# First expert layer of a two-layer graph network: order of the scatters, of SP's row loads and of the sort's lookups

## What is computed

```python
H = gelu(xf @ W1 + b1)                       # 6250 x 1024
probs = softmax(H @ Wg + bg)                 # 8 experts
assign = argmax(probs, axis=-1)
for e in range(8):
    y = H @ Wd[e] + bd[e]
    out = out + where(assign == e, probs[:, e:e+1] * y, 0)
```

## Time and profile before

| what | us |
|---|---|
| median of 3 runs | 10559.74 (10548.85 to 10565.69) |
| the profiled execution, its time | 10558.26 |
| its span in the profile | 10556.3 |
| of it: self-loops on POOL | 3936 to 4022 |
| groups | 4022 to 4888 |
| positions and rows into XS | 4888 to 4984 |
| tiles | 4984 to 6071 |

### The profile page before, as it was taken

The page is one execution under the profiler, slowest core; times in us unless marked ns, Lnnn a source line. Parts: engine busy times, 40 slices in busy tenths (PEclk is TensorE's granted clock), DMA queues, the critical chain, the costliest instruction groups (busy, mean ns, idle before and its releaser), DMA issues. The chain is left out here.

```text
span 10556.3 us, 132376 instructions
## 1 busy us (share of the span) xinstructions
PE 6743.9 (64%) x29670; PEld 5088.8 (48%) x29671; DVE 4968.9 (47%) x10855; ACT 3051.4 (29%) x7313; POOL 6031.6 (57%) x6341
## 2 busy tenths in 40 slices
PE   4674999999999755775777665555444463555530
PEld 2333666666666544664666634444333352344420
DVE  6875777777777774664444431111111121222224
ACT  1113666656666201111111113333333310111110
POOL 1223666666666106666444537777777716777763
PEclk8777999999999876776777777777777666777765
DMA  2115666666777332222444334443333322222214
GB/s 74 51 55 175 209 208 208 208 207 208 208 209 210 97 93 61 71 72 84 124 124 125 108 115 119 118 119 112 100 100 100 101 61 55 43 48 45 47 28 152
DMA packets 657558, 1228.01 MB, mean 116 GB/s; under 512 B 165551, under 2 KB 409475, under 8 KB 657254
## 3 DMA queue, kind: packets, MB, share of 16 engines
q0 software_dynamic: 301872, 718.92, 24.7%
q1 hardware_dynamic: 327959, 467.65, 14.1%
q10 hardware_dynamic: 27580, 39.79, 1.0%
HBM read 1088.88 MB, written 145.05 MB: 117 GB/s over the span
## 5 line engine op out<-in xcount | busy, mean ns | idle before, releaser
L948 POOL DMA_INDIRECT e_kv<-KV,e_idx x1712 | 1634.2, 955 | 756.2 <-issue 482.4
L2453 POOL DMA_INDIRECT s_x<-XN,s_idx x1712 | 1622.7, 948 | 589.8 <-issue 499.4
L1593 POOL DMA_INDIRECT SD<-o_pay,o_pos x1024 | 1077.8, 1053 | 806.7 <-DVEq L45 438.3
L2510 PE MATMUL s_psA<-s_x,s_oh 128*128 128x256 f32 x1712 | 665.0, 478 | 1112.7 <-DMA s_x<-XN,s_idx 1018.9
L2868 POOL DMA_INDIRECT t_g<-G,t_idx x1088 | 1077.1, 990 | 329.7 <-issue 329.7
L2546 DVE TENSOR_TENSOR NS<-s_psA,NS 128x256 f32 x856 | 363.4, 425 | 1743.9 <-PE s_psA L2511 1743.5
L1053 PE MATMUL e_psQ<-QA,e_oht 128*128 x3424 | 895.0, 407 | 200.5 <-issue 102.1
L2510 PEld LDWEIGHTS s_psA<-s_x,s_oh 128*128 128x128 f32 x1712 | 405.7, 245 | 1222.2 <-issue 1152.5
L1053 PEld LDWEIGHTS e_psQ<-QA,e_oht 128*128 128x128 f32 x3424 | 646.9, 199 | 368.9 <-issue 282.4
L3036 PE MATMUL t_psH<-t_xT,t_w 128*128 128x384 f32 (+1 forms) x1088 | 425.5, 558 | 379.0 <-ACT t_H L3013 358.5
L2511 PE MATMUL s_psA<-s_x,s_oh 128*128 128x256 f32 x1712 | 625.0, 453 | 0.0
(11 more groups left out here) (580 smaller groups left out, 12617.4 us busy)
## 6 DMA issues: line engine op xcount, KB each, us to landing
o_dbf<-DBF SPq DMA_DIRECT2D x128, 512.0 KB
f_w<-in_L_ffn_Wd_dram SPq DMA_DIRECT2D x57, 1024.0 KB
e_relb<-REL SPq DMA_DIRECT2D x107, 512.0 KB, 6.0
o_dlo<-DLO SPq DMA_DIRECT2D x128, 256.0 KB
e_kv<-KV,e_idx POOLq DMA_INDIRECT x1712, 3.9
s_x<-XN,s_idx POOLq DMA_INDIRECT x1712
YD<-t_y ACTq DMA_DIRECT2D x50, 512.0 KB, 2.7
mx_y<-YD SPq DMA_DIRECT2D x10, 2560.0 KB, 11.3
```

The costliest lines, as they stand in the source:

```text
L948: pool.indirect_dma_start(kv[:, s, t, :], None, k.KV, bass.IndirectOffsetOnAxis(ap=idx[:, s, t:t + 1], axis=0)).then_inc(kv_in[s][g], 16)
L1593: pool.indirect_dma_start(self.k.SD, bass.IndirectOffsetOnAxis(ap=self.pos[:, s, j:j + 1], axis=0), self.pay[:, s, j, :], None).then_inc(s ...
L2453: pool.indirect_dma_start(x[:, s, t, :], None, k.XN2, bass.IndirectOffsetOnAxis(ap=idx[:, s, t:t + 1], axis=0)).then_inc(x_in[s], 16)
L2510: pe.matmul(psA[:, u % 4, 0:C], oh[:, o, 2 * u, :], x[:, s, 2 * u, :], start=True, stop=False)
```

## The change

Four edits, all in `GatSort` and `first_experts`:

1. The 64 self-loop scatters leave `pool_start`. A new method `place(pool, t)` issues one of them; 7 are issued after the groups, one after each sort block of the 57 tiles. The wait for their landing moves to `pool_end`.
2. In the tile loop POOL issues `give(j-2)` ahead of the sort block's scatters rather than behind them. The loop is now 57 tiles written out, not a hardware loop (`place` takes its column at build time).
3. SP reads `xa` one tile earlier: `xa` of tile j+1 is asked for at the head of SP's work for tile j, ahead of the sort's broadcasts.
4. In a group the seven sort steps of PE stand after the transposes, after m = 1, 3, 5 and 7, within the logits (after the third of five node tiles) and after the logits; ACT's steps follow.

```diff
@@ -1582,10 +1582,10 @@
         for s in range(2):
             pool.dma_start(self.blank[:, s, 1:2], self.blank[:, s, 0:1]).then_inc(self.scattered[s], 16 * SB)
         pool.wait_ge(self.loops_done, 1)
-        for t in range(HG):
-            pool.indirect_dma_start(k.SD, bass.IndirectOffsetOnAxis(ap=k.start2_i[:, t:t + 1], axis=0),
-                                    self.loops[:, t, :], None).then_inc(self.placed, 16)
-        pool.wait_ge(self.placed, 16 * HG)
+
+    def place(self, pool, t):
+        pool.indirect_dma_start(self.k.SD, bass.IndirectOffsetOnAxis(ap=self.k.start2_i[:, t:t + 1], axis=0),
+                                self.loops[:, t, :], None).then_inc(self.placed, 16)
 
     def pool_step(self, pool, b, s):
         after(pool, self.pos_done, b)
@@ -1594,6 +1594,7 @@
                                     self.pay[:, s, j, :], None).then_inc(self.scattered[s], 16)
 
     def pool_end(self, pool):
+        pool.wait_ge(self.placed, 16 * HG)
         for s in range(2):
             pool.wait_ge(self.scattered[s], 16 * SB * (self.blocks // 2 + 1))
 
@@ -1844,16 +1845,22 @@
             sp.wait_ge(owner_done, 1)
             sp.wait_ge(sorted_, 16 * NT)
 
-            def fetch(j, s, e):
+            def load_xa(j, s):
                 at(sp, xb_done, j - 2, 1, 0)
                 sp.dma_start(xa[:, s, :], rows(k.XS, j)).then_inc(xa_in[s], 16)
+
+            def fetch(j, s, e):
                 at(sp, out_done, j - 2, 1, 0)
                 sp.dma_start(xs[:, s, :], rows(k.XS, j)).then_inc(xs_in[s], 16)
                 sp.dma_start(b2[:, s, :], w["L0_ffn_bd"][bass.ds(e, 1), :].rearrange("a n -> (a n)").partition_broadcast(P)).then_inc(xs_in[s], 16)
                 at(sp, y_ps, j - 2, 1, 0)
                 sp.dma_start(w2[:, s], w["L0_ffn_Wd"][bass.ds(e, 1), :, :].rearrange("a (m p) n -> p (a m) n", p=P)).then_inc(w2_in[s], 16)
 
+            load_xa(0, 0)
+
             def body(j, s):
+                if inside(j + 1):
+                    load_xa(j + 1, 1 - s)
                 sort.sp_step(sp, *tile_slot(j, s))
                 e = nc.values_load_multi_w_load_instructions(
                     owner[0:1, bass.ds(j, 1)], engines=[mybir.EngineType.SP], min_val=0, max_val=EX0 - 1,
@@ -1878,6 +1885,8 @@
                         power(g + 1)
                     sort.pool_step(pool, *slot(g, s, n))
             groups(pool, body)
+            for n in range(HG - NB):
+                sort.place(pool, n)
             pool.wait_ge(zeroed, 16)
             pool.wait_ge(pos_done, 1)
             for t in range(NT):
@@ -1889,11 +1898,11 @@
                 pool.indirect_dma_start(k.X2, bass.IndirectOffsetOnAxis(ap=oidx[:, s:s + 1], axis=0), xo[:, s, :], None)\
                     .then_inc(kept[s], 16)
 
-            def body(j, s):
-                sort.pool_step(pool, *tile_slot(j, s))
-                if not isinstance(j, int) or j > 1:
-                    give(j - 2, s)
-            tiles(pool, body)
+            for j in range(NB):
+                if j > 1:
+                    give(j - 2, j % 2)
+                sort.pool_step(pool, *tile_slot(j, j % 2))
+                sort.place(pool, HG - NB + j)
             for j in range(NB - 2, NB):
                 give(j, j % 2)
             sort.pool_step(pool, GatSort.blocks - 1, (GatSort.blocks - 1) % 2)
@@ -2043,13 +2052,16 @@
                         after_step(act, hp_done, g, HS, -1)
                     act.activation(xT[:, :, i0 * P:(i0 + n) * P].rearrange("p a (i n) -> p i a n", n=P), psT[:, 0:n], ACT.Copy)\
                         .then_inc(tc_done, 1)
+                sort.act_step(act, *slot(g, s, 0))
                 for m in range(MH):
                     for h in range(2):
                         after_step(act, hp_done, g, HS, 2 * m + h)
                         act.activation(H[:, m, h * HALF:(h + 1) * HALF], psH[:, h, 0:HALF], ACT.Gelu,
                                        bias=b1[:, m:m + 1]).then_inc(h_done, 1)
-                    if m < BG:
-                        sort.act_step(act, *slot(g, s, m))
+                    if m % 2:
+                        sort.act_step(act, *slot(g, s, (m + 1) // 2))
+                for n in range(MH // 2 + 1, BG):
+                    sort.act_step(act, *slot(g, s, n))
             sort.act_start(act)
             groups(act, group)
             act.wait_ge(lx_done, 1)
@@ -2087,6 +2099,7 @@
                         for a in range(KC):
                             last = pe.transpose(psT[:, i, a, :], xn[:, i0 + i, a * P:(a + 1) * P], k.ident[:])
                     last.then_inc(tp_done, 1)
+                sort.pe_step(pe, *slot(g, s, 0))
                 after_step(pe, tc_done, g, TR, TR - 1)
                 for m in range(MH):
                     for h in range(2):
@@ -2095,14 +2108,17 @@
                             last = pe.matmul(psH[:, h, 0:HALF], w1[:, a, m * P:(m + 1) * P], xT[:, a, h * HALF:(h + 1) * HALF],
                                              start=(a == 0), stop=(a == KC - 1))
                         last.then_inc(hp_done, 1)
-                    if m < BG:
-                        sort.pe_step(pe, *slot(g, s, m))
+                    if m % 2:
+                        sort.pe_step(pe, *slot(g, s, (m + 1) // 2))
                 after_step(pe, h_done, g, HS, HS - 1)
                 after(pe, l_done, g - 1)
                 for i in range(GT):
                     for m in range(MH):
                         last = pe.matmul(psL[:, i, :], H[:, m, i * P:(i + 1) * P], wg[:, m, :], start=(m == 0), stop=(m == MH - 1))
+                    if i == GT // 2:
+                        sort.pe_step(pe, *slot(g, s, BG - 2))
                 last.then_inc(lg_done, 1)
+                sort.pe_step(pe, *slot(g, s, BG - 1))
             sort.pe_start(pe)
             groups(pe, group)
             pe.wait_ge(oh_done, 1)
```

## The result

The changed kernel takes 10116.7 us (median of 4 runs, 10101.4 to 10120.1) against 10562.7 us before: a ratio of 0.9572, with a 95% interval of 0.9559 to 0.9584. That is 446 us less by the medians, where 470 were forecast, and within the range given.

What follows compares the result with a forecast made beforehand. POOL was taken to bound the groups, broken once per group, and DVE's loop with its wait for `xa` the tiles. Gains 72 + 89 + 3 + 2 + 304 = 470 us from 10558.3 gave 10088 us, range 10062 to 10185.

Steps and rivals of the forecast that it cites:

- Self-loops out of the start: Stage start: without 64 self-loops POOL starts 68.0 us earlier, and PE's earlier first lookup adds 4; gain 72 us.
- Lookups spread: Groups: spreading PE's lookups closes POOL's nine gaps at group boundaries; gain between 0 and 90 us, taken as 89.
- Seven self-loops behind the groups: After the groups: 9.3 us of self-loops fill POOL's 12.05 us idle wait for `pos_i`; gain 3 us.
- The way to the first tile: Before the tiles: SP puts `xa` of tiles 0 and 1 ahead of the broadcasts; 0 to 4 us, taken as 2.
- The tiles: Tile loop: the period falls from 18.88 to 13.55 us over 57 tiles; gain 304 us.
- Step 5: Tile loop: give ahead of the scatters, `place` behind; moved give counted at nothing, POOL 13.42 us per tile.
- step 4's loop: Tile loop: with `xa` a tile ahead its 5.58 us wait goes, leaving DVE's loop at 13.56 us, lookup at half clock.
- B: Rival, chance 0.14: PE paces the tiles at 14.4 to 15 us, losing 48 to 83 us; near 10155 us.
- C: Rival, chance 0.06: the group gap stays in another slot, the lookup within the logits waiting for `hots_done`; 89 lost, 10177 us.
- D: Rival, chance 0.06: the weights or `kept` replace the wait for `xa`; tile 16 to 17 us, 10230 to 10285 us.
- E: Rival, chance 0.03: `xa`, asked for in time, still comes late among the broadcasts; tile near 18.9 us, 10390 us.
- F: Rival, chance 0.03: slower, as DMA instructions in POOL's straight-line tile code wait for their code; 10598 us at 22.5 per tile.

Runs made afterwards that it cites:

- xa_alone_2: The kernel before with only SP's earlier read of `xa`, on a chip like the result's: 10453.4 us, ratio 0.9917, tile 17.16 us.
- give_alone_2: The kernel before with only the give moved ahead of the sort block's scatters, hardware loop kept: 10526.2 us, ratio 0.9989, tile 18.53 us.
- no_loops: The changed kernel with the 64 self-loops back in `pool_start` and POOL's tiles again in a hardware loop: 10086.6 us, ratio 0.9564.
- no_spread: The changed kernel with PE's and ACT's old group order: 12349.5 us (0.9861) on a slow chip, 10165.4 us (0.9645) on one like the result's.

## Why the prediction was right, and where it was not

The direction, the size (446 of 470 us) and the mechanism (POOL nearly back to back from the first block to the last) held. Step by step, by the traces, which have 453:

1. *Self-loops out of the start*: forecast 72, measured 71.2. "Blocks 1 and 2 come at DVE's pace, under the 10.8 us of POOL" was wrong: block 1 came 9.5 us late (counted in the groups). The step overlooked what stands on SP's queue before block 2's broadcast, a fill of 7.6 MB whose effect the removed self-loops had hidden.
2. *Lookups spread*: forecast 89, measured 68.8 (865.5 to 796.7). The nine gaps did go. What was given back is the 9.5 us of point 1, 0.012 us on each of 560 scatters (6.8 us), and 3.5 us in four pauses with nothing to wait for, one in each turn of POOL's loop of two groups (1.6 to 3.9 us each, before 0.6 to 2.2). Edit 4 taken out alone is worth 60 us of the stage, not 89.
3. *Seven self-loops behind the groups*: forecast 3, measured 2.9. The way to the first tile gave 5.5 us, not 2.
4. *and 5. The tiles*: forecast 304, measured 309.3. The sum was right, its shares were not. Step 5 counted the moved give at nothing because "most of it lay beside the lookup"; xa_alone_2 and give_alone_2 show a second loop of 17.2 us under the first of 18.5 to 18.9, so the give is worth about as much as `xa`: given the other edit, 17.16 - 12.14 = 5.0 us a tile against 18.53 - 12.14 = 6.4. The sentence read a mean wait of 1.9 us per tile as slack, and it was the distance between two loops of nearly one length. And step 4's loop of 13.56 us was taken as the bound; it was POOL's 13.42 (measured 13.45), and that the wrong bound lay 0.1 us beside the right one is luck. no_loops ran at 12.14 us a tile, so DVE's loop is no longer than that on average. One record of the lookup took 0.41 us on average in the tiles before, 0.32 in the changed kernel and 0.29 in no_loops: the half clock in step 4's loop went with the idling.
6. *The end* was not in the sum: 4.4 us lost, cause open.

Of the signs, two were off: the first row scatter came at 4750.5 and not near 4740, for the reasons of point 2, and DVE's wait for the lookup in the tiles did not stay but fell from 82.5 to 49.2 us.

Of the rivals, B (PE paces) fell: PE's mean clock rose to 0.88, and to 0.93 at 12.14 us a tile, as its case against said. C fell with the idling of 18.6 us. D and E fell with 4.4 us of waiting for `xa` in 57 tiles, though D's `kept` is what xa_alone_2 ran into without edit 2. F fell: written out alone, POOL's tiles cost 0.12%. The Trainium skill's rule (SBUF — State Buffer, "SBUF: two separate sides"), by which the `tensor_scalar` of `xa` could have cost its length on POOL, did not show: the give and the scatter at 5204.95 and 5206.31, beside it, took 1.06 and 0.97 us, and the mean scatter of the tiles was 1.038 us against 1.053. Over all tiles the 33 instructions of POOL that lay beside this `tensor_scalar` took 0.98 us on average and 1.18 at most. Whether it runs in a two-port mode no run here shows. Nor was the overlap new, as the prediction had it: before the change 50 instructions of POOL lay beside it and took 0.97 us.

What the forecast did not ask is what a part of the change is worth against the rest. The 57 self-loops were priced into the tile's period, correctly, but with DVE's loop of 13.56 thought to stand over it they seemed free. They are not: edit 1 gives 71 us at the start and takes 75 back in the tiles.

## What to carry to other kernels

Before a wait is priced, close the second-longest loop as well: follow the chain from an event to its own next occurrence through every engine, and take the longest that remains, since cutting the longest wins only the distance to the next (here 1.7 of 18.9 us) until both are cut. Work moved off a start into a loop is free only on an engine that idles there after the change, so look for a stage in which that engine has nothing to do. When work that filled a stretch is removed, list what else was under its cover, the big DMA in front of a small one first.

## What the runs showed of the hardware

Two things were not expected. A chip differed from the others by 19% for the same program (12532 against 10540 to 10563 us), with instructions of the same length and 160 against 207 GB/s in the window shown, and on it the groups with the old order of lookups idled 253 to 274 us against 79 to 93. A ratio measured there is not the ratio elsewhere: the same kernel, no_spread, had 0.9861 and a tile of 17.18 us on it, and 0.9645 and 13.44 us on another. And a DMA issue on SP, 0.33 us in the tiles, took 9.37 us while the 7.6 MB fill was under way (10.96 in the kernel before); in the kernels with the fill in three pieces no issue in this stage took over 3.5 us.
